# One tap of the last convolution formed on ScalarE and added on GpSimd, VectorE's two other taps behind it

## The reference

```python
# block 1: windowed attention beside a 3x3 depthwise convolution
x1 = layernorm2d(x)                         # over the 96 channels
q, k = split(conv1x1(x1, qk_w)); vs = conv1x1(x1, vs_w)
local = conv2d(vs, depth_w, 'SAME', groups=96) + depth_b
y = concat([window_attention(q, k, vs[:, :48]), vs[:, 48:]], 1)
ca = sigmoid(conv1x1(leaky_relu(conv1x1(mean(y + local), fu1_w)), fu2_w))
z = conv1x1(y * ca + local * (1 - ca), proj_w) + x
# block 2: a 3x3 depthwise convolution whose filter is formed per image
t = relu(batchnorm(mean(z) @ w1.T)); wt = (t @ w2.T + b2) * MASK
out = conv2d(z, wt, padding=1, groups=4 * 96) + bias
```

## Time and profile before

| what | us |
|---|---|
| median of 3 runs (1414.25 to 1417.43) | 1415.69 |
| the profiled execution | 1415.28 |
| its span | 1413.6 |
| PE busy | 1303.9 (92%) |
| DVE busy | 1174.8 (83%) |
| ACT busy | 953.1 (67%) |
| POOL busy | 398.3 (28%) |

### The profile page before, as it was taken

One profiled execution on the slowest core, in us unless ns is written; L12 is line 12 of the kernel. 1 busy time (PEld: TensorE's weight loads), 2 busy tenths in 40 slices (PEclk: granted clock), 3 DMA queues, 4 the chain that ended last, 5 costly groups with the idle time before them and its releaser, 6 DMA issues.

```text
span 1413.6 us, 38309 instructions
## 1 busy us (share of the span) xinstructions
PE 1303.9 (92%) x12403; PEld 773.8 (55%) x12403; DVE 1174.8 (83%) x2028; ACT 953.1 (67%) x2375; POOL 398.3 (28%) x870
## 2 busy tenths in 40 slices
PE   5999999899999999999999999989999999679995
PEld 3666667655555555555555555555555555323331
DVE  3566656579999999999999999999999999779996
ACT  2576766777777777787777777777777777533332
POOL 3121211123333333333333332333333332111111
PEclk9999999999999999999999999999999999899998
DMA  2122222455666766666666655665667665568995
GB/s 66 51 86 64 80 68 76 111 132 138 151 161 171 164 154 155 150 166 153 149 160 171 169 154 150 151 166 148 158 152 174 165 155 149 132 156 209 222 228 135
DMA packets 81364, 203.13 MB, mean 144 GB/s; under 512 B 15248, under 2 KB 19112, under 8 KB 81320
## 3 DMA queue, kind: packets, MB, share of 16 engines
q1 hardware_dynamic: 72424, 176.65, 47.8%
q0 software_dynamic: 7168, 25.17, 9.6%
q10 hardware_dynamic: 1728, 0.79, 0.2%
HBM read 136.57 MB, written 64.91 MB: 143 GB/s over the span
## 4 chain that ended last, share of the span: by engine, by line
PE 36%; DVE 22%; DMA 15%; ACT 13%; issue 9%; ACTq 2%; SPq 1%; POOLq 0%; DVEq 0%; POOL 0%
DMA zs<-in_x 12%; DVE mixed L1273 7%; PE banks_g L532 7%; PE banks_s L557 5%; PE banks_g L645 5%; DVE mx L1099 4%; ACT zs L904 4%; PE banks_t L591 3%; ACT vd L843 3%; DMA ycat<-y_img 3%; PE banks_g L540 3%; DVE oo L1285 3%; DVE xn L1092 3%; PE banks_t L565 2%; DVE bn L1071 2%
## 5 line engine op out<-in xcount | busy, mean ns | idle before, releaser
L1273 DVE SCALAR_TENSOR_TENSOR mixed<-vin,c_pack,mixed 96x1024 f32<-96x1024 f32 x352 | 451.1, 1282 | 8.6 <-ACT mixed L893 1.6
L1285 DVE SCALAR_TENSOR_TENSOR oo<-zs,l_w,oo 96x1016 f32<-96x1016 f32 x192 | 243.8, 1270 | 46.4 <-ACT oo L914 42.5
L447 POOL COPY vrow<-vw 96x16 f32<-96x16 f32 (+2 forms) x520 | 265.2, 565 | 0.0
L467 POOL TENSOR_TENSOR rest<-rest 96x1 f32<-96x1 f32 x64 | 38.5, 601 | 605.4 <-ACT zs L904 605.4
L1099 DVE TENSOR_REDUCE mx<-banks_s 128x16 f32<-128x1024 f32 x130 | 158.4, 1218 | 23.1 <-PE banks_s L557 22.0
L1071 DVE BATCH_NORM_STATS2 bn<-banks_a 128x6 f32<-128x96 f32 x528 | 99.7, 251 | 85.1 <-PE banks_a L507 84.7
L557 PE MATMUL banks_s<-km,qd 64*128 64x128 f32 x2080 | 152.9, 287 | 14.5 <-DVE mx L1099 12.8
L557 PEld LDWEIGHTS banks_s<-km,qd 64*128 64x128 f32 x2080 | 128.4, 189 | 67.4 <-ACT qd L827 34.6
L645 PE MATMUL banks_g<-vin,proj_t 128*96 128x512 f32 (+1 forms) x288 | 149.0, 618 | 13.4 <-DMA ycat<-y_img 6.6
L867 ACT ACTIVATE pt<-banks_t 128x512 f32<-128x512 f32 x256 | 137.6, 589 | 34.8 <-PE banks_t L565 34.8
L565 PE MATMUL banks_t<-qd,km 64*128 64x128 f32 x2048 | 150.5, 287 | 3.3 <-DMA qd<-nmx 3.3
(11 more groups left out here) (151 smaller groups left out, 1817.4 us busy)
## 6 DMA issues: line engine op xcount, KB each, us to landing
vin<-v_img SPq DMA_DIRECT2D x64, 495.0 KB, 5.6
v_img<-vrow SPq DMA_DIRECT2D x130, 198.0 KB, 2.7
xc<-in_x SPq DMA_DIRECT2D x134, 192.0 KB, 7.0
zs<-in_x POOLq DMA_DIRECT2D x64, 384.0 KB, 8.7
out<-oo SPq DMA_DIRECT2D x64, 384.0 KB, 3.5
y_img<-ybuf SPq DMA_DIRECT2D x128, 99.0 KB, 2.0
ycat<-v_img SPq DMA_DIRECT2D x64, 198.0 KB, 4.9
ycat<-y_img SPq DMA_DIRECT2D x64, 198.0 KB, 7.9
```

The lines of the kernel that those rows point to most:

```text
L447: nc.gpsimd.tensor_copy(dst.rearrange("c r (p x) -> c p r x", x=min(WS, src.shape[-1])), src).then_inc(vrow_done, 1)
L1273: v.scalar_tensor_tensor(out=mb[:C, par, :, 0:W], in0=vin[:C, par, 1 + dh:1 + dh + WS, 1 + dw:1 + dw + W], scalar=depth_w[:, DVE_TAPS[m]:D ...
L1285: v.scalar_tensor_tensor(out=oo[:, par, :, to], in0=zs[:, par, 1 + dh:1 + dh + WS, of], scalar=l1_w[:, tap:tap + 1], in1=oo[:, par, :, to] ...
```

## The change

Tap 3 of block 2 (the pixel to the left) is taken from VectorE. ScalarE forms the product into a new buffer `part` (`tap_part`), behind `tap0`, and GpSimd adds it to `oo` (`add_part`, both operands in SBUF). VectorE's two taps that are left wait for that sum (`part_added`), no longer for `tap0`. In the steps with attention VectorE's first tap moves from between the two maxima to behind `divide` 1, and `mix` 5 takes its place.

```diff
-L1_REST = (0, 2, 3)
+L1_REST = (0, 2)
+L1_PART = 3
...
+            def add_part(u, par):
+                pool.wait_ge(part_done, u + 1)
+                dh, dw = L1_TAPS[L1_PART]
+                to = oo[:, par, :, -dw:W]
+                nc.gpsimd.tensor_tensor(to, to, part[:, :, -dw:W], ALU.add).then_inc(part_added, 1)
...
                 if attend:
                     to_image(t + 1, 1 - k, h + k)
+                if prev and not late:
+                    add_part(t - LAG - 1, k)
+                if late:
+                    add_part(t - LAG - 2, 1 - k)
+                if attend:
                     wrap(t + 2)
...
+            def tap_part(u, par):
+                act.wait_ge(part_added, FREE + u)
+                dh, dw = L1_TAPS[L1_PART]
+                fn(part[:, :, -dw:W], zs[:, par, 1 + dh:1 + dh + WS, 0:W + dw], ACT.Copy,
+                   scale=l1_w[:, L1_PART:L1_PART + 1]).then_inc(part_done, 1)
...
                     tap0(u - 1, h - NS // 2 - 1, k, after)
+                    tap_part(u - 1, k)
...
                 if n == 1:
-                    dve.wait_ge(tap_done, FREE + u + 1)
+                    dve.wait_ge(part_added, FREE + u + 1)
...
-                if prev:
-                    l1(u - 1, k, 1)
-                if attend:
-                    maxima(t + 1, 1)
                 if cur and not tail:
                     mix(u, par, 5, tail)
+                if attend:
+                    maxima(t + 1, 1)
...
                 if prev:
-                    l1(u - 1, k, 2)
+                    l1(u - 1, k, 1)
```

More of the change, by code:

```diff
@@ L243, in program @@
         tap_done = sem("tap_done")
+        part_done = sem("part_done")
+        part_added = sem("part_added")
         l1_step = sem("l1_step")
@@ L469, in add_x, with strip @@
                                accum_op=ALU.add).then_inc(x_added[par], 16)
-            def strip(h, k, attend=True, prev=True):
+            def add_part(u, par):
[3 more added lines that the diff above has]
+                nc.gpsimd.tensor_tensor(to, to, part[:, :, -dw:W], ALU.add).then_inc(part_added, 1)
+            def strip(h, k, attend=True, prev=True, late=False):
                 t = 2 * h + k
@@ L492, in _ @@
                     strip(h, k)
-            with pool.Fori(B * NS // 2, B * NS // 2 + NS // 2 + 1) as h:
+            h0 = B * NS // 2
+            for k in range(2):
+                strip(h0, k, attend=False)
+            add_x(2 * h0 + 1 - LAG, 0)
+            strip(h0 + 1, 1, attend=False, late=True)
+            with pool.Fori(h0 + 2, h0 + NS // 2 + 1) as h:
                 for k in range(2):
-                    strip(h, k, attend=False)
+                    strip(h, k, attend=False, late=True)
+            add_part(B * NS - 1, 1)
         @block.tensor
@@ L1005, in strip @@
                     tap0(u - 2, h - NS // 2 - 2 + k, 1 - k, before)
+                    tap_part(u - 2, 1 - k)
                     halo(u - 1, k)
@@ L1056, in _ @@
             tap0(B * NS - 2, B * NS // 2 - 1, 0)
+            tap_part(B * NS - 2, 0)
             halo(B * NS - 1, 1)
             tap0(B * NS - 1, B * NS // 2 - 1, 1)
+            tap_part(B * NS - 1, 1)
         @block.vector
@@ L1310, in last @@
                 u, par = 2 * h + k - LAG, 1 - k
+                if old:
+                    for n in range(1, NL + 1):
+                        l1(u - 3, 1 - par, n)
                 for m in range(NT):
                     mix(u, par, m, True)
-                if old:
-                    for n in range(1, NL + 1):
-                        l1(u - 2, par, n)
             def strip(h, k, attend=True, cur=False, prev=False, gate=None, gated=None, tail=False):
@@ L1346, in strip @@
                     squeeze_in(gate)
-                if prev:
-                    l1(u - 1, k, 1)
+                if cur and not tail:
+                    mix(u, par, 5, tail)
                 if attend:
                     maxima(t + 1, 1)
-                if cur and not tail:
-                    mix(u, par, 5, tail)
                 if gate is not None and not attend:
@@ L1395, in _ @@
             last(h0 + 1, 0, old=False)
-            last(h0 + 1, 1)
+            last(h0 + 1, 1, old=False)
             with dve.Fori(h0 + 2, h0 + NS // 2) as h:
@@ L1400, in _ @@
             last(h0 + NS // 2, 0)
-            for u in (B * NS - 2, B * NS - 1):
+            for u in range(B * NS - 3, B * NS):
                 for n in range(1, NL + 1):
```

4 lines of the change are left out of this document (3 added, 1 removed).

## The result

The changed kernel takes 1425.91 us in the median of 8 runs (1419.02 to 1428.22), the kernel before, beside it, 1416.56 (1411.72 to 1420.69). The ratio, formed from all runs and not from the two medians, is 1.0055 with a 95% interval of 1.003 to 1.008: slower by 7.8 us (the medians differ by 9.35), a little less than the forecast 9.5. The profiled execution took 1419.23 us, so it is one of the short ones.

What follows compares the result with a forecast made beforehand. Steps with attention were taken to alternate between the `x` landing loop and TensorE's order; loads and TensorE set later strips. Terms 3.5 + 0.5 + 1.06 + 1.6 + 0.7 + 2.1 = 9.5 on 1415.28: 1424.8 us, range 1411 to 1432.

Steps and rivals of the forecast that it cites:

- The closed loop from landing to landing: Late-landing attention steps: landing, `tap0`, tap, maxima, L571, `nmx`, ScalarE's list, `z_out`, DMA; `tap0` to `z_out` 7.95, then 7.90 us.
- my line through two small additions: GpSimd's addition, extrapolated from additions of 1 and 32 elements (192 and 249 ns): 2.06 us, taken 2.1.
- I take a landing of 11.78 us in all of them: Steps with attention: earlier loads make `x` land late in every step; 19.71 instead of 19.62 us, times 39: +3.5 us.
- cover, not path: Steps with attention: VectorE's saved tap shortens nothing, since `mix` 5, as long, stands where the tap stood.
- That of 0.22: Rival beside attention: earlier loads empty the queue sooner, late steps vanish; -6.6, total 1414.7 us, no measurable change; chance 0.22.
- That of 0.18: Rival beside attention: VectorE's freed time gives back 0.3 us in each of 39 steps; -11.7, total 1409.6 us; chance 0.18.
- The last gate: ScalarE's sums stand behind `tap_part`, +1.06; next step, landing to SP's store takes 7.65 instead of 6.02 us, +1.6.
- Strips without attention: After the last gate: the freed 1.3 us goes to GpSimd's hold, nothing gained, at worst 2.9 lost; taken +0.7 us.
- The hold E: Without attention: GpSimd's addition holds VectorE 1.7 to 2.3 us a strip, 13 times; costs time from E = 2.08.
- the rival of 0.15: Rival without attention: the hold decides, at E = 2.5 losing 5.5 instead of 0.7; total 1430 us; chance 0.15.
- The end: Behind the last landing, serial: `tap_part` 1.06, addition with semaphores 2.3, two taps 2.59, instead of three taps 3.89: +2.1 us.
- the signs that I had named: Profile signs: addition near 2.1, little idle before `nmx`, no L571 wait, loads near `z_out`, landing about 11.8, 3 us taps without attention.

Runs made afterwards that it cites:

- the three kernels with the added wait: Beside attention SP's loads wait for the end of the previous strip's `z_out`: in the changed kernel 0.9960, the kernel before 0.9962, the order alone 0.9917.
- the two profiles of the changed kernel: The changed kernel measured twice, the second time with no edit: ratios to the kernel before 1.0055 and 1.0033; profiled executions 1419.23 and 1424.06 us.
- the order alone: Kernel before with, beside attention, VectorE's three taps behind `mix` 5 and the second maxima, nothing on ScalarE or GpSimd; measured twice: ratios 0.9957 and 0.9923.
- the copy: The order alone plus ScalarE's `tap_part` behind `tap0` beside attention, its output added by nobody, and one VectorE wait at the gates: ratio 1.0014.
- the two kernels with the old order and taps beside attention: The kernel before, and the kernel before with the new tap only from the last gate on (ratio 1.0051).
- the maxima last: The order alone with the first of VectorE's three taps back in front of the second maxima, `mix` 5 still ahead of both: ratio 1.0123.
- the squeeze first: Changed kernel with the small operations of `squeeze` ahead of VectorE's taps at the last gate: ratio to the kernel before 1.0049.

## Why the prediction was right in sign, and where it failed

**What bounds the kernel** was read rightly. The closed loop from landing to landing exists and has its predicted length: 7.96 us from `tap0` in the step above, against 7.90. The steps without a late landing mostly last 19.30 and 19.54 us in every kernel that has the maxima ahead of the taps of block 2, with time to spare on ScalarE before `nmx`. Two readings were loose: 19.62 us is the average of the first eleven steps (all 37 give 19.58), and the loads start less than 0.55 us behind `z_out` in 12 of those 37, with `x` 0.57 us later there.

**The new pieces.** `tap_part` took 1.13 us (1.15 predicted). The addition took 2.32 to 2.34 in 41 of the 64 strips, the last one with VectorE idle among them, and 2.56 to 2.65 in strips behind the last gate; I had kept 1.9 to 2.4 and taken 2.1. From the figure of the Trainium skill's page GPSIMD Engine Reference, section 3.1, I had estimated 2.4, and the trace agrees with that more than with my line through two small additions.

**Steps beside attention: the sign was wrong.** The step that failed is "I take a landing of 11.78 us in all of them". VectorE's taps did end sooner and the loads did start sooner, 0.10 us behind `z_out` on average instead of 0.71. But `x` landed at 11.15 us on average (11.20 before), and late in 5 and 6 steps instead of 11. I had drawn a line through loads at +0.2 and +0.8 and extended it below them. That loads at +1.4 bring an earlier landing is right, as the three kernels with the added wait show (10.24, 10.88 and 10.98 against 11.15, 11.20 and 11.37); that loads ahead of `z_out` bring a late one is not. In the two profiles of the changed kernel the loads start ahead of `z_out` in 35 of 74 steps: `x` lands there at 10.99 us on average and never late, against 11.34 and 11 late landings in the 39 others. This is a pattern, which no run tried by itself.

The second half of the error is that I called VectorE's order "cover, not path". The order alone is worth 6 to 11 us, by its ratios. I had seen L571's wait, and had even let it go in the working; but I set ScalarE's `tap_part` in its place in every step at once, and so never priced the two separately: the order gives some 5 to 9 us in this stage (885.14 and 883.88 against 890.31 and 892.52), and with the copy all of it goes again (892.50); in the changed kernel, where `x` lands late less often, about half of it goes (887.7 on average). So two rivals were each right in part. That of 0.22, loads with a head start, fits the landings just told, but the late steps did not vanish and -6.6 was too much. That of 0.18 named waits such as L571's, and the order alone shows that they are worth something; but it was the order that took them away, mostly in the late steps, and -11.7 was too much.

**The last gate.** Predicted +2.7, measured +3.6 in the first profile and +2.0 between the means. The way from landing to SP's store came out as worked: from 1247.13 to 1255.03 it is 7.90 us, against 7.65 predicted (the terms listed add to 7.67) and 6.02 before. What I had not seen is that TensorE waits there too, behind the squeeze, which stands behind the tap in VectorE's list. That the loss stayed near my figure is luck: the next strip's loads are late anyway and hide part of it.

**Strips without attention.** Predicted +0.7, measured +3.1. The hold E was sized well: a strip of 9.61 us less 5.22 and 2.59 leaves 1.80 (1.7 to 2.3 predicted, with 2.08 as the point from which it should cost). The failed term is that point. I spread the free time of 15 strips, 139.0 us, evenly; part of it lies in waits for loads behind the last gate (ScalarE's `first` waits 2.43 us for `vin` at 1270.28) and can't be used later. Behind the 51st `z_out` the kernels without the new tap take 121.9 / 13 = 9.38 us a strip, so 9.61 costs at once, 13 x 0.24 = 3.1: the point lies at 9.38 - 5.22 - 2.59 = 1.57, not 2.08. That is the mechanism of the rival of 0.15, with a smaller E. No row before showed VectorE held for long; now one `mix` of 3.24 us instead of 1.28 does, so it was held for 1.96 of the addition's 2.6 us. The Trainium skill's page SBUF — State Buffer, section Who interferes with whom, says that a VectorE instruction with two SBUF inputs contends with a GpSimd one that reads SBUF, and that the shared ports are an exclusive lock; the trace agrees with it.

**The end** was right: +2.1 predicted, 2.05 measured. In the rows the last two taps start 1411.46 - 1406.75 = 4.71 us behind `tap0`:

```profile
1406.75 1.24 ACT L936 ACTIVATE oo<-zs,c_pack,l_w 96x1024 f32<-96x1024 f32 x1 [3.33 <-DMA zs<-in_x]
...
1411.46 2.58 DVE L1317 SCALAR_TENSOR_TENSOR oo<-zs,l_w,oo 96x1016 f32<-96x1016 f32 x2 [3.22 <-POOL oo L479]
```

Taken together by stages, with the mean of the two profiles of the changed kernel (887.7) against that of the two kernels with the old order and taps beside attention (891.4): -3.7 + 2.0 + 3.1 + 2.05 = 3.4 us. The two ratios give 7.8 (4.2 to 11.3) and 4.7 (1.7 to 7.7). The second holds it, the first does not quite; where the rest of the first lies, in the start or in executions that no profile caught, stays open. That the total is near the forecast is partly luck: the steps beside attention came out 7.7 us below their term, and the strips without attention 2.4 above theirs. Its sign is not luck alone, since the last gate, the strips and the end each lost, as forecast.

Of the signs that I had named, five came: `nmx` with little idle time, no wait for the maxima, loads close to `z_out`, an addition little over 2.1 us, and taps of 3.2 us without attention (the fourth of `mix` in each strip). One did not: landings at 11.8 us. Of the two points at which I had called myself wrong, steps of 19.4 were nearly reached, with 19.48 and 19.51, and an addition over 2.5 us was reached beside a busy VectorE, with 2.65.

## What to carry to other kernels

A change that moves one instruction past others has two parts, the work that is moved and the order that is left behind; run the order alone before you pay for the move, since here it was the whole gain, and the move cost it again. Keep an instruction that waits for late data behind those whose results others wait for, in every in-order list: the maxima ahead of the tap, as shown here, and the squeeze ahead of the tap, which helped its own strip but not measurably the whole run. And look for free time strip by strip where the work repeats; an average over a stage counts time that can't be carried along.

## What the runs showed of the hardware

The moment at which SP's loads are queued moves the landing of another queue's DMA: the one added wait, to 1.4 us behind `z_out`, moved the mean landing from 11.15 to 10.24 in the changed kernel, from 11.20 to 10.88 in the kernel before, and from 11.37 and 11.62 to 10.98 in the order alone. Below that it goes in no one direction, in kernels that differ in other things too: loads at -0.18 (the maxima last) came with 11.22, at about 0.1 with 11.15 to 11.23, at 0.2 (the squeeze first) with 11.29, at 0.35 (the order and the copy) with 11.43, at 0.55 (the order alone) with 11.37 and 11.62, at 0.7 to 0.8 (the old order) with 11.20 and 11.38. Why was not tried.

In the changed kernel GpSimd's smallest work is held as well: its addition of one element for the `x` DMA (L471) took 0.19 us in the last strip, at 1401.20, and 1.28 at 1343.51, where VectorE adds taps without a pause.

The same code of a gate step ran at the lower clock in one profile and not in another. In the profile with the squeeze first, whose code at the first inner gate is that of the changed kernel, TensorE was idle for 0.70 us up to 607.04 and for 1.35 up to 609.55; from 609.59 on its granted clock was 0.5 for 17.1 us, and the step took 28.07:

```profile
608.39:636.46 28.07, 26.50 (x183) 15.52 (x184) 17.90 (x39) 18.70 (x45) 7.41 (x14) 0.70 0.48 117
```

In the changed kernel's profile the same step took 22.34 us at a granted clock of 1.00; there TensorE was idle for 0.96 us at that place.
